# Graph layers on one core: one-hot products over 128 rows, reordered evictions and statistics, tile 0's products ahead of its scores

## The reference

```
h = max(layernorm(x), 0)
# layer 0: attention over edges
hw = h @ W + b_w
s_dst, s_src = hw @ a[:512], hw @ a[512:]
e = leaky_relu(s_dst[dst] + s_src[src] + b_a, 0.2); w = exp(e)
alpha = w / segment_sum(w, dst)[dst]
x = x + segment_sum(alpha[:, None] * hw[src], dst)
# layer 1: four experts, two SAGE layers each, the best two of them added by their gates
h = max(layernorm(x), 0)
h_e = relu(mean_of_neighbours(h_e) @ Wl[e, l] + bl[e, l] + h_e @ Wr[e, l])   # l = 0, 1
x = x + sum of top-2 gates * h_e
```

## Time and profile before

| | us |
|---|---|
| median of 3 runs | 745.5 (745.43 to 745.51) |
| the profiled execution | 744.08 |
| its span | 742.3 |
| TensorE busy | 717.8 |
| VectorE busy | 428.0 |
| ScalarE busy | 398.1 |

### The profile page before, as it was taken

The page is one execution under the profiler, slowest core; times in us unless marked ns, Lnnn a source line. Parts: engine busy times, 40 slices in busy tenths (PEclk is TensorE's granted clock), DMA queues, the critical chain, the costliest instruction groups (busy, mean ns, idle before and its releaser), DMA issues.

```text
span 742.3 us, 12047 instructions
## 1 busy us (share of the span) xinstructions
PE 717.8 (97%) x3574; PEld 582.2 (78%) x3574; DVE 428.0 (58%) x1056; ACT 398.1 (54%) x897; POOL 184.1 (25%) x204
## 2 busy tenths in 40 slices
PE   5899999999999999999999999999999999999994
PEld 3589977888888888777777777878888888888883
DVE  8899889999752538622722622657444544444341
ACT  6966769677653521511511511347677667767751
POOL 4000000000000100850300010045666555655511
PEclk9999999999999999999999999999999999999998
DMA  9100000111501247799699695379844994438950
GB/s 207 39 4 3 4 3 18 53 35 35 165 8 58 79 123 240 217 333 326 228 354 328 200 359 197 99 184 264 300 93 88 264 343 120 86 69 225 290 156 6
DMA packets 46444, 115.19 MB, mean 155 GB/s; under 512 B 8340, under 2 KB 8552, under 8 KB 46361
## 3 DMA queue, kind: packets, MB, share of 16 engines
q1 hardware_dynamic: 28581, 77.60, 32.7%
q0 software_dynamic: 9136, 19.65, 11.6%
q10 hardware_dynamic: 8644, 16.86, 6.9%
HBM read 64.89 MB, written 50.08 MB: 155 GB/s over the span
## 4 chain that ended last, share of the span: by engine, by line
PE 92%; DVE 4%; ACT 1%; issue 1%; POOL 0%; DVEq 0%; ACTq 0%; POOLq 0%
PE ps L1783 16%; PE ps L1784 16%; PE ps L1785 16%; PE ps L2185 7%; PE ps L2184 6%; PE ps L2052 3%; PE ps L2053 3%; PE ps L1985 3%; PE ps L1860 3%; PE ps L1979 3%; PE ps L1980 3%; PE ps L2115 2%; PE ps L1923 1%; PE ps L1811 1%; PE ps L1925 1%; PE ps L1924 1%
## 5 line engine op out<-in xcount | busy, mean ns | idle before, releaser
L1110 ACT ACTIVATE agn<-ps,rec 32x128 f32<-32x128 f32 x336 | 120.7, 359 | 38.7 <-PE ps L2185 34.8
L1044 ACT ACTIVATE slots<-he_t 125x512 fp32r<-125x512 f32 x40 | 25.3, 635 | 150.9 <-DVE he_t L1581 146.6
L2185 PE MATMUL ps<-slots,CTs 125*128 x230 | 89.9, 391 | 0.0
L1581 DVE TENSOR_TENSOR he_t<-ps,b_b 125x512 f32<-125x512 f32 x40 | 27.6, 691 | 105.5 <-PE ps L1785 72.3
L728 POOL DMA_INDIRECT hrow<-t_d,piece_i x80 | 76.1, 951 | 25.7 <-issue 23.5
L2184 PE MATMUL ps<-slots,CTs 125*128 x207 | 80.7, 390 | 0.0
L1746 DVE TENSOR_TENSOR tm<-ps,b_b 128x512 f32<-128x512 f32 x23 | 15.9, 692 | 84.3 <-PE ps L1785 84.2
L1783 PE MATMUL ps<-W,agT_hi 128*125 128x512 f32 x160 | 63.5, 397 | 0.0
L1783 PE MATMUL ps<-W,h2T_hi 128*125 128x512 f32 x160 | 63.4, 396 | 0.0
L1785 PE MATMUL ps<-W,agT_lo 128*125 128x512 f32 x160 | 63.3, 396 | 0.0
L1784 PE MATMUL ps<-W,agT_hi 128*125 128x512 f32 x160 | 63.2, 395 | 0.0
(11 more groups left out here) (316 smaller groups left out, 1665.4 us busy)
## 6 DMA issues: line engine op xcount, KB each, us to landing
he_d<-slots SPq DMA_DIRECT2D x30, 448.0 KB
slots<-he_d SPq DMA_DIRECT2D x30, 448.0 KB
w_d<-slots SPq DMA_DIRECT2D x3, 4096.0 KB, 18.7
slots<-w_d SPq DMA_DIRECT2D x24, 512.0 KB
t_d<-he_t SPq DMA_DIRECT2D x40, 224.0 KB
raw<-in_L_gnn_Wl ACTq DMA_DIRECT2D x4, 1024.0 KB, 7.2
raw<-in_L_gnn_Wr ACTq DMA_DIRECT2D x4, 1024.0 KB, 5.6
slots<-in_L_gnn_Wl ACTq DMA_DIRECT2D x4, 1024.0 KB, 10.0
```

What stands on the lines that cost most here:

```text
L1110: last = a.activation(agn[32 * r:32 * r + 32, q, :], ps[n, 3 + i % 2, 128 * r:128 * r + 128], ACT.Copy, scale=rec[n, i, 4:5])
L2185: last = mm(o, CTs[:, t, :], part(k, P, t * 1024 + D, P), start=False, stop=t == T - 1)
```

## The change

1. `e_q`, `q_row`, `q_at` and `q_sel` get 128 rows in place of 65; the added rows of `q_row`, so of `q_sel`, are zero, and those of `e_q` one. The products of the hot blocks then run over 128 rows with the same result.
2. TensorE starts with `wake`: 12 f32 products of `ones` and `ident` into bank 7, whose result is not used.
3. VectorE's block is block 3, not 2. `spread_spans` stands behind block 3 (was 2), `turn_edges` behind 4 (3), `sum_tables` behind 9 (7), `turn_tables` behind 10 (8), the product that covers bank 6 behind 11 (9). On ScalarE, `e_gc` moves from block 3 to block 5, `columns(0)` from 10 to 13; `W0_hi` is copied behind block 15, `bias_in(0)` behind 17, `norm(0)` behind 18.
4. VectorE's row statistics: none ahead of its block, one row each in the waits of the table, the rest behind it. Tile 0's two registers are loaded while the late statistics run.
5. `scales()` stands behind the first 5 of tile 0's one-hots. `W0_lo` and `hT_lo` stand ahead of `sources()`, which end with the two sums over the bias, after `wa`.
6. TensorE runs tile 0's 12 products ahead of its scores, sorted by operand (`hT_hi` x `W0_hi`, `hT_lo` x `W0_hi`, `hT_hi` x `W0_lo`), and `scores(0)` waits for `wa` alone. ScalarE waits for `s_add` ahead of `nat_hi` of tile 0, since that overwrites `a_b`, and for `scores(0)` ahead of `hT_hi` of tile 1.

The core of the diff:

```diff
-        e_q = at("e_q", [2 * CR + 1, CG, P], F32R, 15040)
+        e_q = at("e_q", [128, CG, P], F32R, 15040)
...
-        q_sel = at("q_sel", [2 * CR + 1, CR, P], F32R, R1 + 20480)
+        q_sel = at("q_sel", [128, CR, P], F32R, R1 + 20480)
...
-        HOT_DVE = (2,)
+        HOT_DVE = (3,)
...
             def product_high(t):
                 act.wait_ge(*hw_done(t + 1))
+                if t == 0:
+                    act.wait_ge(*wa_ready(2))
...
                 if b > 0:
                     act.wait_ge(*hw_done(b))
+                if b == 1:
+                    act.wait_ge(*s_done(1))
...
+                if u == 15:
+                    act.wait_ge(*w0_in(16))
+                    copy(W0_hi[:], W0_f[:]).then_inc(w0_hi_ready.sem, 1)
                 if u == 16:
                     act.wait_ge(*var_ready(1))
                     a.activation(std[:], std[:], ACT.Sqrt).then_inc(std_ready.sem, 1)
-            act.wait_ge(*norm_ready(1))
-            norm(0)
-            act.wait_ge(*w0_in(16))
-            copy(W0_hi[:], W0_f[:]).then_inc(w0_hi_ready.sem, 1)
+                if u == 17:
+                    bias_in(0)
+                if u == 18:
+                    act.wait_ge(*norm_ready(1))
+                    norm(0)
...
+            v.memset(q_row[2 * CR:, :], 0.0)
...
+            row_stats(range(2, T // 2))
             dve.wait_ge(*x_late_in(32))
-            link(row_stats(range(T // 2, T)))
+            late = row_stats(range(T // 2, T))
+            dve.wait_ge(*flag_ready(2))
+            dve.wait_ge(*tab_ready(1))
+            first_flags = batch_flags(0)
+            link(late)
...
                     last.then_inc(step_ready.sem, 1)
+                    if b == 0 and k == 0:
+                        scales()
...
                 else:
-                    scales()
-                    sources()
+                    first_weights_low()
                 if b < T - 1:
                     turned_low0(b)
                 if b == 0:
-                    first_weights_low()
+                    sources()
...
+            def wake():
+                pe.wait_ge(*consts(2))
+                for _ in range(12):
+                    mm(ps[:, 7, 0:128], ones[:], ident[:], start=True, stop=True)
+
+            wake()
...
                 if b == 0:
-                    pe.wait_ge(*wa_ready(2))
+                    pe.wait_ge(*wa_ready(1))
...
-                scores(b)
-                if b == 0:
-                    pe.wait_ge(*w0_lo_ready(1))
+                if b > 0:
+                    scores(b)
                 pe.wait_ge(*bias_ready(b + 1))
                 o = ps[0:P, 6, :]
+                if b == 0:
+                    pe.wait_ge(*hT_hi_ready(1))
+                    for c in range(KC):
+                        first = mm(o, hT_hi[:, c], W0_hi[:, c], start=False, stop=False, skip_group_check=True)
+                        if c == 0:
+                            first.then_inc(batch_done.sem, 1)
+                    pe.wait_ge(*hT_lo_ready(1))
+                    for c in range(KC):
+                        mm(o, hT_lo[:, c], W0_hi[:, c], start=False, stop=False, skip_group_check=True)
+                    pe.wait_ge(*w0_lo_ready(1))
+                    for c in range(KC):
+                        last = mm(o, hT_hi[:, c], W0_lo[:, c], start=False, stop=c == KC - 1, skip_group_check=True)
+                    last.then_inc(hw_done.sem, 1)
+                    scores(0)
+                    return
```

More of the change, by code:

```diff
@@ L1191, in hot_columns, with batch_flags @@
                                 ).then_inc(hot_dve_ready.sem, 1)
+            def batch_flags(b):
+                more = more_here(dve, b)
+                return more, dve.value_load(tab_b[0:1, b:b + 1, BW + 1:BW + 2], min_val=0, max_val=NW * NG)
             def row_stats(tiles):
@@ L1196, in row_stats @@
                 return last
-            dve.wait_ge(*x_in(32))
-            row_stats(range(0, 2))
             hot_columns(HOT_DVE[0])
@@ L1218, in _ @@
             v.tensor_scalar(tab_f[:, 1:2], tab_f[:, 1:2], -1.0, None, ALU.add).then_inc(n_ready.sem, 1)
-            row_stats(range(2, 4))
+            dve.wait_ge(*x_in(32))
+            row_stats(range(0, 1))
             dve.wait_ge(*n_summed(1))
             v.tensor_copy(tab_f[:, 2:3], ps[0:NW, 7, 0:1]).then_inc(tab_f_ready.sem, 1)
-            row_stats(range(4, T // 2))
+            row_stats(range(1, 2))
             dve.wait_ge(*tab_turned(1))
@@ L1257, in sources @@
                 source_vectors(1)
-                for w in range(2):
-                    dve.wait_ge(*wa_f_ready(2 * KC - 1 + w))
-                    v.scalar_tensor_tensor(spill[w][0:P, :], bw_b[:], 1.0, a_b[0:P, w, :], ALU.mult, ALU.mult,
-                                           accum_out=ab[:, w:w + 1]).then_inc(ab_ready.sem, 1)
                 dve.wait_ge(*wa_f_ready(2 * KC))
@@ L1264, in sources @@
                 v.tensor_tensor(wa[:, :, 2:4], wa_f[:], f32(wa[:, :, 0:2]), ALU.subtract).then_inc(wa_ready.sem, 1)
+                for w in range(2):
+                    v.scalar_tensor_tensor(spill[w][0:P, :], bw_b[:], 1.0, a_b[0:P, w, :], ALU.mult, ALU.mult,
+                                           accum_out=ab[:, w:w + 1]).then_inc(ab_ready.sem, 1)
                 dve.wait_ge(*ab_ready(2))
@@ L1288, in tile_and_batch @@
             def tile_and_batch(b):
-                more = more_here(dve, b)
-                before = dve.value_load(tab_b[0:1, b:b + 1, BW + 1:BW + 2], min_val=0, max_val=NW * NG)
+                more, before = batch_flags(b) if b > 0 else first_flags
                 dve.wait_ge(*column_ready(b + 1))
```

32 lines of the change are left out of this document (16 added, 16 removed).

## The result

The changed kernel takes 747.59 us, the median of 20 runs from 746.75 to 756.97, and the kernel before 745.48 us, the median of 20 runs from 744.71 to 746.92. The ratio is 1.0048 with a 95% interval of 1.0031 to 1.0065. It is slower, clear of the 0.2% in which I had put the forecast: 745.5 us and "no change". Nine of the 20 runs lie between 746.75 and 747.25, 1.3 to 1.8 us above the kernel before. The profiled execution took 746.88 us and is one of the nine.

A forecast was written before the change was run, and what follows sets the result against it. TensorE bounds the kernel, with VectorE level at tile 1's scores. Root at 27.86, VectorE's 13.66, waits 0.1 and 1.1, and read-out 0.08 put tile 1's one-hots at 42.8 against 42.82: shift 0.0, so 745.5 us, range 744.7 to 748.7.

The forecast's parts named there:

- no change: Whole kernel: time within 1.5 us of the kernel before, which its runs can't tell apart; chance 0.75.
- S: Start of VectorE's one-hots of tile 1; forecast 42.8 us against 42.82 before, with tile 1's scores 6.14 us later.
- std_ready: ScalarE's square root handed back to VectorE ahead of the scales; forecast at 27.86 us, including 0.55 of idle time.
- scales, 20 one-hots, `W0_lo` (from there): VectorE's work in tile 0 after the root: 0.3 for scales, 3.96 for one-hots, 2.2 for W0_lo.
- wait for `hT_hi`: VectorE's wait after W0_lo (done at 34.3) until ScalarE ends hT_hi of tile 0 at 34.45; put at 0.1 us.
- source group with read-out, `s_add` whole: VectorE's source vectors at tile 0's end: 6.6 us for the group plus 0.08 for the accumulator's read-out.
- bare loads and branch: VectorE's idle time ahead of tile 1's one-hots, from flag register loads; put at 1.1 us, ends 0 and 1.33.
- A cover that is gone: VectorE, end of tile 0: tile 1's register loads lose W0_lo's 2.28 us cover and stand behind s_add; price 1.1 us.
- falls only during the hot blocks: Rival: TensorE's clock falls there and rises in tile 0's counts, delaying hT_hi by 0.4 us; 745.9, inside the forecast's 0.60.
- The twelve products: TensorE's start: twelve products from 3.1 to 8.3 us cost nothing and have the clock at the upper level from 9 us.
- The clock around tile 1: Rival: TensorE, working in pieces after 39 us, drops to 1.2 GHz, costing about 3 us; 748.5 us, chance 0.12.
- the new wait and the bare loads cost nothing: Rival: no idle time on ScalarE and flag loads fully hidden on VectorE, S at 41.0; 743.7 us, chance 0.05.

The follow-up runs named there:

- e8_before_delayed: Kernel before with 14 needless 512-column products on TensorE ahead of tile 3's transposes; 747.18 us against 743.98, ratio 1.0038.
- e15_delayed_short: Kernel before with 3 needless products on TensorE ahead of tile 3; 744.73 us, ratio 1.0007.
- e3_flags_early: Changed kernel with tile 1's register loads moved up beside tile 0's, under the late statistics; 744.63 us against 743.98 for the kernel before.
- e12_sources_ahead: Changed kernel with the sources again ahead of hT_lo and W0_lo on VectorE; 746.78 us, ratio 1.0029 to the kernel before.
- e9_cover_last: As e6_combined, but bias sums last and s_add behind tile 1's first five one-hots; 743.56 us against 745.54 for the kernel before.
- e2_no_wake: Changed kernel without the 12 products ahead; 748.68 us against 743.98 for the kernel before, ratio 1.006.
- e1_before_clock_part: Kernel before with the 12 products ahead and 128 rows in the hot blocks, nothing reordered; 742.46 us against 743.98, ratio 0.9984.
- e13_wake_65_again: Kernel before with the 12 products ahead only, 65 rows kept, on a third quiet chip; 742.67 us against 744.02, ratio 0.9985.
- e6_combined: Changed kernel with early register loads, bias sums in the root's wait, root ahead of W0_hi, hT_lo between the source halves; 742.67 us against 743.98 for the kernel before.
- e10_wake_65_rows: Kernel before with the 12 products ahead only, 65 rows kept, where before takes 745.5; 748.24 us against 745.54, ratio 1.0022.
- e7_combined_pool: As e6_combined, with W0_lo made by GpSimd instead of VectorE; 745.18 us against 743.98 for the kernel before, ratio 1.0019.
- e16_rows_alone: Kernel before with 128 rows in the hot blocks and without the 12 products; 743.89 us, ratio 0.9995.
- e5_changed_again: The changed kernel once more, on a second chip; 745.43 us against 743.98 for the kernel before, ratio 1.0018.

## Why the prediction was wrong

*What bounds the kernel, and S as the key: right.* The table above says that the time is S plus a constant for each of the two groups, over about 4 us of S and eleven kernels. Tile 1's scores stand at S + 6.20 (I had 6.14). TensorE's saving at tile 0 was given back at tile 1, as forecast: 2.05 us of waiting and counts that take 4.80 us, paced by the one-hots. `e8_before_delayed` and `e15_delayed_short` show that a shift there reaches the end whole.

*The size of S: wrong, 44.27 for 42.8, and this is the step that failed.* By the terms of the sum (the sixth, `hT_lo` at 0.6, was right):

| step | predicted | measured | late by |
|---|---|---|---|
| `std_ready` | 27.86 | 28.35 | 0.49 |
| scales, 20 one-hots, `W0_lo` (from there) | 6.46 | 6.56 | 0.10 |
| wait for `hT_hi` | 0.1 | 0.31 | 0.21 |
| source group with read-out, `s_add` whole | 6.68 | 6.92 | 0.24 |
| bare loads and branch | 1.1 | 1.53 | 0.43 |

"A cover that is gone" was the right mechanism and the largest of the errors: with `s_add` in the open it is 0.67 us. I took 1.1 and set the upper end at 1.33, from tile 0's loads. But those stood behind no branch. The branch at the end of tile 0 is in the diff's order listing, in both kernels, and I gave it no price; before, the loads and it together lay under `W0_lo`. The rest, 0.24, is `s_add` and its wait for the sums. `e3_flags_early` parts loads and branch (0.94 and 0.59), `e12_sources_ahead` puts the cover back, and `e9_cover_last` shows that two sums without a wait behind them do as well. The range that I gave the term was therefore not a bound: loads behind a branch cost more than the like elsewhere.

`std_ready` was late because ScalarE waited 0.50 and 0.41 us where I allowed 0.55 in all, and started 0.11 later; the root's whole length, 0.30, counts too, where I took 0.15. (The terms of ScalarE's work add up to 15.80, not to the 15.85 of the prediction.) The wait for `hT_hi` was the one named under "falls only during the hot blocks": the clock did fall, at about 25.7, and the transposes ran at 1.2 GHz. No term erred by more than 0.5 us, but all five erred the same way, and my window for "no change" was 1.5 us on either side of a sum whose errors could all point up. Every value was chosen as if nothing else would stand in the way. My own sign of being wrong, tile 1's one-hots after 44.3, was so wide that 44.27 just passes it. With S 1.45 us later than before, the way in which I carried the shift over gives 746.95, and the nine short runs take 746.75 to 747.25. A chance of 0.75 for "no change" was too high for a sum of new exposures with nothing on the other side.

*The twelve products: right, and undervalued.* The clock was up at 9 us, `e2_no_wake` puts 1.46 us of S on it, and `e1_before_clock_part` and `e13_wake_65_again` show that on their own they make the kernel before 1.35 to 1.5 us faster. I had counted the faster blocks only as the way to an early root. They also bring `std` itself 1.46 us sooner, and in the order before that is worth 1.45 us of S. The changed order gives it away, because it makes VectorE wait for ScalarE's root (1.40 us), with 1.8 us of `W0_hi` put ahead of it. By S, the twelve products gave about 1.4 us, and the rest of the change took about 2.9 (an estimate from 41.37, 42.82 and 44.27).

*The clock around tile 1: half right.* It fell (0.58 in 46 to 50 us), at no cost here, since only paced counts lay under it. In `e1_before_clock_part` a fall at tile 0's products cost 1.56 us. That the wider gap near the end had left the clock up proved nothing for this place. Tile 0's counts ran at 1.2 GHz too, so TensorE ended tile 0's products at 42.3, not at 39.2, and this also cost nothing.

*The rival "the new wait and the bare loads cost nothing": the right idea, with 743.7.* It didn't happen in the changed kernel. `e6_combined` fills the wait and hides the loads, and `e9_cover_last` hides the branch too; they gain 1.3 and, in eight of twelve runs, about 2.2 us.

*What stays open: the long runs.* On the chip of the first series and on that of `e9` to `e12`, a third to two thirds of the runs of every kernel with the 12 products are 1 to 10 us longer than its shortest kind, and of the kernel before none of 55 is more than 1.6 above its median. It isn't the order of the front or the row count, since `e10_wake_65_rows` has it with neither. The one long run that was profiled has it near 490 us in layer 1, as a wait of 7.8 us without a named releaser. On three other chips no run is more than 2.4 us above the shortest of its kernel, those of `e13_wake_65_again` included; but `e1_before_clock_part`, `e2_no_wake` and `e7_combined_pool` have two kinds of runs there, some 1 to 2.3 us apart, of which only one was profiled each time. The delayed kernels, which shift the same work by 0.7 and 3.2 us, ran only on quiet chips, so they don't tell whether a mere shift in time would bring it out. That the transfers of layer 1 meet something else in time is an argument, not a finding.

## What to carry to other kernels

Where an instruction moves away from the end of a loop body, look at what the sequencer does behind it: a branch and register loads, here 1.5 us, were free only under a long instruction with no wait behind it. Where two engines reach a point together, as the earlier trace rows show, only the later of them counts, so a saving on one has to be matched on the other before it is worth anything. And an error bar that comes from a look-alike row holds only if everything around that row is alike.

## What the runs showed of the hardware that I had not expected

- A branch whose own record is 0.06 us long left VectorE idle for 0.59 us (`e3_flags_early`) and 0.70 us (`e6_combined`) where no longer work covered it, and the register loads of one tile took another 0.94.
- 16 us of products on 65 rows, TensorE busy for 79 to 100% of each stretch, left the clock at 0.50 (`e10_wake_65_rows`, 15 to 31 us); on 128 rows it stayed at 1.00 from 9 to 24 us with 2.2 to 3.0 us busy of each 3.0 (the changed kernel). The kernel before and `e16_rows_alone` differ in the rows alone, and with 128 the spacing is that of the upper level from 21 us on, with 65 not before the counts. But 128 rows don't always hold it: in `e1_before_clock_part` it read 0.60 from 18 to 21 us and 0.50 from 21 to 24, after a stretch of 3 us with 1.20 us busy, and in `e5_changed_again` 0.63 from 15 to 18. When it rises without the 12 products differs: at about 13 us in `e2_no_wake`, at about 21 us in `e16_rows_alone`.
- The granted clock reads 1.00 in the kernel before while spacing says 1.2 GHz (0.43 us for 512 columns), but reads 0.50 once it has fallen after being up. Before the first rise only spacing told here.
- One GpSimd instruction of 4.53 us held up one of VectorE's 16-bit one-hots for its whole length, 4.56 us in place of 0.28.
- The same program takes 744.0 us on some chips and 745.5 in other series. Four profiles of reordered kernels from the latter have a wait of TensorE for `hT_f` of 0.8 to 1.5 us near 492 to 496 us, which the profiled run of before has not; of the kernel before no profile was taken there.
